# A group's softmax denominators are applied by ScalarE and GpSimd instead of VectorE, and the two steps behind run two places later

## What is computed

```python
Q = linear(Q_cat, qproj_w, qproj_b).reshape(b_, l_, H, DK).transpose(0, 2, 1, 3)
K = linear(K_cat, kproj_w, kproj_b).reshape(b_, l_, H, DK).transpose(0, 2, 1, 3)
V = linear(x, Wv_w, Wv_b).reshape(b_, l_, H, DK).transpose(0, 2, 1, 3)
scores = jnp.einsum('bhqd,bhkd->bhqk', Q, K) / sqrt(DK)
scores = scores * tau[..., None] + delta[:, :, None, :]
attn = jax.nn.softmax(scores, axis=-1)
out = jnp.einsum('bhqk,bhkd->bhqd', attn, V)
out = out.transpose(0, 2, 1, 3).reshape(b_, l_, D)
return linear(out, out_w, out_b)
```

## Time and profile before

| | |
|---|---|
| median of 3 runs | 1506.13 us (1504.74 to 1506.78) |
| the profiled execution | 1506.3 us, span of its instructions 1504.6 us |
| TensorE busy | 1307.4 us, 87% |
| VectorE busy | 1206.0 us, 80% |
| ScalarE busy | 1056.2 us, 70% |
| GpSimd busy | 682.8 us, 45% |

### The profile page before, as it was taken

How to read it: one execution, slowest core, us unless ns; L and a number is a source line. 1 busy time by engine, 2 the same in 40 slices (tenths; PEclk the granted TensorE clock), 3 DMA queues, 4 the chain that set the end, 5 groups by cost and what they waited for, 6 DMA issues and landing times.

```text
span 1504.6 us, 22722 instructions
## 1 busy us (share of the span) xinstructions
PE 1307.4 (87%) x8452; PEld 508.3 (34%) x8452; DVE 1206.0 (80%) x1409; ACT 1056.2 (70%) x1836; POOL 682.8 (45%) x716
## 2 busy tenths in 40 slices
PE   5655789889968988886499999999999999999998
PEld 3211334334433433332122222222222222236963
DVE  3999979888988972775699999999999999923522
ACT  5541588677827826453179998999899989997653
POOL 1988868977978856562303114111311132322330
PEclk8767889999988998997689999999999999999999
DMA  8222222222313301420213111100010000010210
GB/s 227 82 81 84 61 89 81 80 65 92 98 57 91 91 21 43 96 47 28 45 31 52 30 30 49 23 2 2 2 23 2 2 2 2 14 39 12 76 31 28
DMA packets 65248, 75.71 MB, mean 50 GB/s; under 512 B 8649, under 2 KB 41290, under 8 KB 65010
## 3 DMA queue, kind: packets, MB, share of 16 engines
q1 hardware_dynamic: 64370, 72.70, 17.9%
q0 software_dynamic: 768, 1.57, 0.4%
HBM read 66.04 MB, written 8.21 MB: 49 GB/s over the span
## 4 chain that ended last, share of the span: by engine, by line
PE 55%; DVE 21%; ACT 10%; issue 7%; POOL 5%; DMA 1%; SPq 0%; POOLq 0%; DVEq 0%; ACTq 0%
PE PS L990 13%; DVE mx L1717 13%; PE PS L978 7%; PE PS L746 5%; PE PS L755 5%; PE PS L947 5%; PE PS L698 2%; PE PS L1062 2%; PE PS L1077 2%; POOL D L1916 2%; PE PS L1098 2%; PE PS L1086 2%; DVE D L1510 2%; ACT D L1218 1%; DVE PS L1489 1%
## 5 line engine op out<-in xcount | busy, mean ns | idle before, releaser
L1355 ACT ACTIVATE aa<-PS 128x512 f32<-128x512 f32 x1024 | 551.6, 598 | 53.3 <-PE PS L978 42.8
L1717 DVE TENSOR_REDUCE mx<-PS 128x2 f32<-128x1024 f32 x480 | 551.8, 1216 | 10.7 <-PE PS L947 7.6
L990 PE MATMUL PS<-aa,D 128*32 128x256 f32 x4096 | 322.2, 392 | 1.5 <-ACT aa L1355 0.6
L978 PE MATMUL PS<-D 54*128 54x512 bf16 x1024 | 212.2, 390 | 10.1 <-ACT aa L1355 8.9
L947 PE MATMUL PS<-D 51*128 51x512 bf16 x960 | 190.2, 385 | 13.6 <-DVE mx L1717 13.1
L2037 POOL CAST n<-nm 4x512 bf16<-4x512 f32 x15 | 9.0, 602 | 404.4 <-ACT nm L1337 404.4
L755 PE MATMUL PS<-xnT,f_w 128*128 128x512 f32 x288 | 158.0, 643 | 7.6 <-ACT HB L1245 6.9
L1489 DVE TENSOR_TENSOR_SCAN PS<-PS,D 128x512 f32<-128x512 f32 x128 | 157.5, 1230 | 7.6
L1245 ACT ACTIVATE HB<-PS 128x512 f32<-128x512 f32 x144 | 84.0, 596 | 105.8 <-PE PS L755 98.7
L746 PE MATMUL PS<-HB,f_w 128*128 128x512 f32 x288 | 147.5, 622 | 6.8 <-DVE GO L1584 5.9
L990 PEld LDWEIGHTS PS<-aa,D 128*32 128x32 f32 x4096 | 84.2, 108 | 196.9 <-issue 156.7
(11 more groups left out here) (356 smaller groups left out, 1720.4 us busy)
## 6 DMA issues: line engine op xcount, KB each, us to landing
D<-bc SPq DMA_DIRECT2D x128, 256.0 KB, 3.5
GB<-gd SPq DMA_DIRECT2D x32, 256.0 KB, 3.7
D<-sc SPq DMA_DIRECT2D x72, 64.0 KB
aa<-in_L_ffn_W SPq DMA_DIRECT2D x9, 256.0 KB, 3.3
D<-in_L_ffn_W SPq DMA_DIRECT2D x9, 256.0 KB, 3.5
f_w<-in_L_ffn_experts_w SPq DMA_DIRECT2D x1, 2048.0 KB, 9.4
f_w<-in_L_ffn_experts_w SPq DMA_DIRECT2D x8, 256.0 KB, 5.9
aa<-gh SPq DMA_DIRECT2D x1, 2048.0 KB, 7.2
```

The costliest lines, as they stand in the source:

```text
L978: e.matmul(take_exp(s + hh), KS[64 * hh:64 * hh + 54, p, 128 * kb:128 * kb + 128], QP[64 * hh:64 * hh + 54, qc % 2, p, :], start=True, sto ...
L990: t = e.matmul(PS[32 * j:32 * j + 32, 7, cs], va[:, kb, 9 * h:9 * h + 32], Pt[K % 3][:, 512 * j + 256 * n:512 * j + 256 * n + 256], start= ...
L1355: e.activation(Pt[K % 3][:, c:c + 512], bank((s + hh) % 3), ACT.Exp).then_inc(S("e_free"), 1)
L1717: e.tensor_reduce(mx4[:, G % 2, b, 2 * pair:2 * pair + 2, c:c + 1], max_banks(m), AX.X, ALU.max).then_inc(freed(m)[0], 1)
```

## The change

`turn` keeps its place on TensorE, but VectorE no longer has a part in it. A new step `scaled` follows at h = 4: ScalarE copies the 144 useful columns of the slot to `tv` in SBUF and frees the slot, and GpSimd computes `rs` as the denominators to the power of minus one and `at` as the product. `heads` waits for these eight counts of `rs` a quarter, and `heads`, `project` and `choose` (with `flip`) come two steps later. `ranks` and `gates` stay at h = 16. The scatters of group 13 stay at their steps.

```diff
         elif h == 3:
             p["turn"](G, maxs.take())
-        elif last and h == 5:
+        elif h == 4:
+            p["scaled"](G)
+        elif last and h == 7:
             p["heads"](q, maxs.take())
-        elif last and h == 7:
+        elif last and h == 9:
             p["project"](q, maxs.take())
-        elif last and h == 12:
+        elif last and h == 14:
             p["choose"](q)
 ...
-        elif G == 13 and h % 2 == 0 and h < 22:
+        if G == 13 and h % 2 == 0 and h < 24:
             p["scatter"](h // 2)
-        elif G == 13 and h == 22:
-            p["scatter"](11)
 ...
+            tv = sa("tv", [128, 4, 4, 9])[:, :, :, :]
+            minus = sa("minus", [128, 16])
 ...
 # TensorE
             def heads(q, m):
                 to = take_max(m)
-                w.wait_ge(*freed(slot["turn"]))
+                w.wait_ge(S("rs"), 8 * q + 8)
 ...
 # ScalarE
+            def scaled(G):
+                m = slot["turn"]
+                w.wait_ge(S("m_full"), m + 1)
+                w.wait_ge(S("rs"), 2 * G)
+                e.activation(tv, max_banks(m)[:, 0, :].rearrange("p (b h c) -> p b h c", b=4, h=4)[:, :, :, 0:9],
+                             ACT.Copy).then_inc(freed(m)[0], 1)
 ...
 # VectorE
-            def turn(G, m):
-                hg = G % 4
-                v7 = max_banks(m)[:, 0, :].rearrange("p (b h c) -> p b h c", b=4, h=4)
-                rv = rs[:, :].rearrange("p (b h o) -> p b h o", b=4, h=4)
-                w.wait_ge(S("m_full"), m + 1)
-                if G:
-                    w.wait_ge(*freed(slot["turn"]))
-                slot["turn"] = m
-                e.reciprocal(rv, v7[:, :, :, 8:9]).then_inc(S("rs"), 1)
-                w.wait_ge(S("rs"), G + 1)
-                e.tensor_tensor(at[:, :, 32 * hg:32 * hg + 32].rearrange("p b (h r) -> p b h r", h=4), v7[:, :, :, 0:8],
-                                rv.to_broadcast([128, 4, 4, 8]), ALU.mult).then_inc(freed(m)[0], 1)
 ...
 # GpSimd
+            def scaled(G):
+                m, hg = slot["turn"], G % 4
+                w.wait_ge(*freed(m))
+                w.wait_ge(S("tabled"), SORT_TABLES + 1)
+                e.tensor_tensor(rs[:, :].rearrange("p (b h o) -> p b h o", b=4, h=4), tv[:, :, :, 8:9],
+                                minus[:, :].rearrange("p (b h o) -> p b h o", b=4, h=4), ALU.pow).then_inc(S("rs"), 1)
+                w.wait_ge(S("rs"), 2 * G + 1)
+                e.tensor_tensor(at[:, :, 32 * hg:32 * hg + 32].rearrange("p b (h r) -> p b h r", h=4), tv[:, :, :, 0:8],
+                                rs[:, :].rearrange("p (b h o) -> p b h o", b=4, h=4).to_broadcast([128, 4, 4, 8]),
+                                ALU.mult).then_inc(S("rs"), 1)
```

More of the change, by code:

```diff
@@ L285 @@
 ATT_IDLE = {name: lambda *_: None for name in (
-    "maxima", "finish", "score", "pv", "evac", "turn", "heads", "project", "choose", "flip", "gates", "up", "down", "fold",
+    "maxima", "finish", "score", "pv", "evac", "turn", "scaled", "heads", "project", "choose", "flip", "gates", "up", "down", "fold",
     "weights", "ranks", "places", "scatter", "stage", "column", "pick", "sorted_up", "sorted_down", "gather", "added")}
@@ L1392, in scalar_program @@
             slot = {}
-            attention_order(ATT_IDLE | dict(finish=finish, score=score, evac=evac, turn=turn, heads=heads, flip=flip,
+            attention_order(ATT_IDLE | dict(finish=finish, score=score, evac=evac, turn=turn, scaled=scaled, heads=heads, flip=flip,
                                             gates=gates, ranks=ranks, sorted_up=sorted_up, up=up))
@@ L1855, in fold @@
                 e.tensor_tensor(xs_, xs_, max_banks(m)[:, 0, :], ALU.add).then_inc(freed(m)[0], 1)
-            attention_order(ATT_IDLE | dict(maxima=maxima, finish=finish, turn=turn, project=project, choose=choose,
+            attention_order(ATT_IDLE | dict(maxima=maxima, finish=finish, project=project, choose=choose,
                                             column=column, pick=pick, score=score, sorted_down=sorted_down, added=added, down=down, fold=fold))
@@ L2045, in finish @@
                 e.tensor_copy(n3[:, 2, :], n2).then_inc(S("n3"), 1)
+            def scaled(G):
[8 more added lines that the diff above has]
+                                ALU.mult).then_inc(S("rs"), 1)
             def turn(G, m):
+                slot["turn"] = m
                 if G:
@@ L2067, in turn @@
                     e.memset(bks[:, b:b + 1], float(b)).then_inc(S("tabled"), 1)
+                e.memset(minus[:, :], -1.0).then_inc(S("tabled"), 1)
             def weights(x):
@@ L2208, in gpsimd_program @@
             slot = {}
-            attention_order(ATT_IDLE | dict(finish=finish, turn=turn, project=project, weights=weights, choose=choose, ranks=ranks,
+            attention_order(ATT_IDLE | dict(finish=finish, turn=turn, scaled=scaled, project=project, weights=weights, choose=choose, ranks=ranks,
                                             places=places, scatter=scatter,
```

## The result

The changed kernel takes 1523.47 us (median of 4 runs, 1521.56 to 1524.31); the kernel before, on the same chip, 1506.04 us (4 runs, 1504.74 to 1506.78). The ratio is 1.0103, with a 95% interval of 1.0081 to 1.0125 (the plain quotient of the two medians, 1.0116, lies inside it). The forecast was 1520.9 us inside 1512.5 to 1524, with slower as the side. The side and the mechanism of the stands held. Several terms were mis-sized, and they partly cancelled.

What follows compares the result with a forecast made beforehand. The chain was taken to run through VectorE for twelve row maxima, then TensorE, with the moved pair off it. Stands of 13.29 us, 14.81 with the clock, on 1506.1 gave 1520.9 us, range 1512.5 to 1524.

Steps and rivals of the forecast that it cites:

- Part 1: VectorE loses reciprocal and multiplication at the turn, hidden behind the L947 matmuls: gain counted as 0, not 8.1 us.
- Part 2: ScalarE's added 128x144 copy at the turn takes 0.29 us and costs 0, with 0.03 us of cover.
- Part 3: GpSimd's added power over 128x16 takes 3.6 us, priced per column, and the multiplication over 128x128 0.40 us.
- Rival B: GpSimd's power is cheap, 1.05 us, its excess paid once: 1513.4 us, or 1514.9 with the clock; 30%.
- Part 4: Quarter ends and tail: `heads` and `project` two steps later, TensorE and gates wait: 6.82, 2.20, 2.24, 1.30 and 0.73 us.
- `heads`, first quarter: End of first quarter: GpSimd's pair queues behind `weights(8)`, so TensorE stands 6.82 us at `heads`.
- `heads`, second and third, each: Ends of second and third quarters: GpSimd is free, its result comes 1.10 us late each time.
- `heads`, tail: Fourth quarter, in the tail: GpSimd's pair stands behind a copy ending at 1381.43, a stall of 1.30 us.
- The clock: TensorE drops to 1.2 GHz after the 6.8 us stand: one stretch of 1.52 us added, two the bound.
- case D: TensorE gets the lower clock twice or more, or also after `ranks`, and part 2's copy is late: 1523.4 us up; 8%.
- A: The forecast case itself, 1518 to 1523 us; 55%.
- C: VectorE's saving of 8.1 us lands: 1505.3 us with B's stalls, 1501 with GpSimd free in the first quarter; 4%.

## Why the prediction was right, point by point

**Part 1, the pair on VectorE: right, with a reason too narrow.** No gain was forecast and none came (37.83 us; with no pair at all 37.83 to 37.84). I named the shadow of the L947 matmuls. The doubled pair showed that the slack is wider: VectorE can be held another 0.40 us at that place for 0.02 us a group. The step that fell short is the reading of the earlier trace rows, where I used the place at which the chain leaves VectorE but not that it stays on TensorE for the next 24 us.

**Part 2, the copy: right.** 0.299 us over 16 copies against an estimated 0.29, and the matmuls that need its banks kept their place. The lines of all 16, durations least, mean and most:

```profile
L2047 POOL TENSOR_TENSOR rs<-tv,minus x16: 2901/2920/3359, 803.8 to 1397.4; 128x16 f32<-128x16 f32 x16
...
L1354 ACT ACTIVATE tv<-PS x16: 297/299/305, 803.5 to 1395.4; 128x144 f32<-128x144 f32 x16
```

**Part 3, the power: right in kind, 0.68 us too dear.** It is paid per column, but with a fixed 0.43 us. I spread the excess of one row of 4 columns evenly over them, and so put the fixed part at 0.20, which is what a cheap operation has. Within 4%, the line is 0.43 + 0.156 a column. Rival B's fixed price is out. The power stays above the 2.50 us from which quarters two and three begin to wait, as they did.

**Part 4, the stands.**

| term | forecast | measured | what the difference is |
|---|---|---|---|
| `heads`, first quarter | 6.82 | 5.12 | -0.67 power; -0.94 below; -0.12 the power started 0.03 before, not 0.09 after, the end of `weights(8)` |
| `heads`, second and third, each | 1.10 | 0.38 | -0.68 power |
| `ranks` | +2.24 | +2.24 | the wait went from 0.74 to 2.98 |
| `heads`, tail | 1.30 | 0.79 | -0.24 power (3.36 here); -0.14 it started 0.05 before the end of the copy ahead; the rest TensorE ready later |
| `gates` | 0.73 | 0.71 | |
| sum | 13.29 | 9.62 | |

The -0.94 is a step that I treated as rigid. `weights(8)` waits for a DMA, and the time from its issue to its landing is not fixed. In after it was issued 2.14 us later than before (913.05 against 910.91), with the attention, and took 3.72 us to land instead of 4.62. So `weights(8)` ended 1.25 us later than before (922.07 against 920.82), and TensorE was ready 2.19 later (920.48 against 918.29). The run with the cheap power saw the difference the other way round (5.09 us). A stand that hangs on a transfer has a spread of its own, 1.4 us in these traces, and the range should have carried it.

**The clock: the term most mis-sized.** I put in one stretch of 1.52 us, and took the stand at `ranks` for too short to matter outside case D. Measured were two stretches of 6.8 us with about 2.8 us each: 7.93 - 5.12 and 5.46 - 2.24 - 0.38. That is 5.6 in place of 1.5. It makes good what the stands fell short: 9.6 + 5.6 + 0.35 for the rest of the tail's 1.85 + 0.1 of plain groups = 15.7. The remaining 2.1 of the span's 17.8 lie before the first turn. In the trace of after, the lower clock at the start of the attention lasted until 768.3 us instead of 764.6. Over the profiled executions the first turn comes anywhere from 797.3 to 806.6 us, and from 798.4 to 806.6 in those whose code ahead of it is that of the kernel before (the latest is the kernel with the six powers, which start at 806.8, behind that turn). So I don't count those 2.1 for the change.

So the sum landed 2.6 us below the median with two errors against each other, -3.7 on the stands and +4.1 on the clock. That they nearly cancel is luck: with the stands as forecast and the clock as measured the time would have been near 1525, outside the range. The case realised is A in its mechanism with the clock of D. The measured 1523.47 also lies just above A's own 1518 to 1523, at D's edge of 1523.4, and D had 8%; its other half, a late copy, didn't occur.

**The rivals.** C, that the saving lands, is refuted by the kernel without a division. B is refuted by the power's price by size, and its reasoning with it: at 0.22 us the kernel is still 0.8% slower. Its premise would not have saved the change, because the queue place decides.

**What stays open.** First, how long the lower clock lasts after a stand: 6.8 us at stands of 5.12, twice 2.98 and 7.13, but 3.4 after 4.08, 3.00, twice 2.99 and 1.73. What it costs is less open. In the changed kernel TensorE works 6.5 us of a 6.8 us stretch at the lower clock, and it costs 2.8. In the kernel with the steps moved the stretch begins 1.2 us before the stand at `ranks` ends, so that TensorE works 5.7 us of it, at a cost of 2.4; in the kernel with the turn in the other bank it works 3.9 us of it, and 49.01 - 40.23 - 7.13 = 1.65 are the cost. With the 1.4 to 1.5 us for a stretch of 3.4, the price is 0.40 to 0.45 us for each microsecond that TensorE works at the lower clock.

Second, single stretches of 3.4 us and 1.5 us of cost appear with no long stand ahead, in 9 of the 13 executions traced and in another group nearly each time (at 1146.9 before, 1280.3 after, 1067.5, 997.8, 991.2, 1225.6, 1338.0 and more, eleven in all). The place within the group is always the same: each begins 1.5 to 2.0 us after the start of a turn's transposes. There TensorE has waited 0.59 us some 2.3 to 2.7 us earlier, and in all but one 0.15 to 0.24 us about half a microsecond earlier. Most turns have the same waits and no such stretch, so what picks the turn is open.

Third, the spread of the time before the attention. None of the three was told apart by an experiment here. Executions of the kernel before that were measured together differ by up to 12 us (1501.6 to 1513.6), and how much of it each makes is not known. For one pair of traces it is: the kernel with the powers, whose groups are otherwise those of before, is 5.7 us longer, 7.2 by its later first turn less 1.5 for the stretch that it lacks.

## What to carry to other kernels

A busy share of 99% doesn't say that an engine's work is on the path: read through which engine the chain runs at the very step where the instruction stands. The same 0.3 to 0.4 us on VectorE cost 0.02 us a group in TensorE's stretch and 0.22 in its own.

Work given to an idle engine takes its place in that engine's queue. Look at what stands ahead of it at the moment its result is needed, and move the consumers of everything that is moved: here the place behind `weights(8)` cost 7.5 us and the unmoved `ranks` and `gates` about 5, while with both mended 4.2 us (0.28%) were left, of which the waits for the new work at `heads` in the second and third quarter were 0.38 us each.

Price a stand of TensorE in an otherwise full stretch with the slow matmuls behind it, here 1.4 to 2.8 us on top of stands of 1.7 to 7.1 us.

## What the runs showed of the hardware

- GpSimd's power over 128 partitions takes, within 4%, 0.43 us and 0.156 us for each column: 0.584, 1.017, 1.637, 2.901, 5.430 and 10.552 us for 1, 4, 8, 16, 32 and 64. Its product over 128x16 took 0.22 us.
- In one execution a stand of 1.73 us was followed, 1.6 us after its end, by 3.4 us at 1.2 GHz; a stand of 1.59 us in the tail of the same execution was not, nor were the waits of 0.38 to 0.79 us at `heads`, `ranks` and `gates`. Eleven single stretches of 3.4 us began 1.5 to 2.0 us after the start of a turn, where TensorE's longest wait just before was 0.59 us. So the one case of 1.73 us is no proof.
- A microsecond of TensorE's work at 1.2 GHz made this kernel 0.40 to 0.45 us longer.
- VectorE's product of two SBUF tiles to 128x128 took 0.29 us in 15 groups and 1.81 us in the one in which a two-input instruction of GpSimd on 128x1024 (2.35 us) ran beside it.
- ScalarE's copy of 128x144 from PSUM took 0.299 us, beside 0.258 for 128x104.
